# A three-part megakernel (attention, routed experts, Mamba): expert sums on GpSimd, one dt tile made in its own batch, two projections in halves

## The chip, the cores and the metric

The kernel runs on one core of a Trainium2 chip, in one launch. The metric is the time of one execution on the device in microseconds; the kernel before took 2910.95 us, the median of three runs (2910.9 to 2911.77).

## The reference, cut to what matters

All of it is float32. `x` has 16 batches of 512 tokens of width 256. The expert layer acts on the first 2048 tokens, that is on the first four batches.

```python
x = x + attention(layernorm(x))
x = x + experts(layernorm(x))     # first 2048 tokens, top 2 of 8, weighted sum of the two results
x = x + mamba(layernorm(x))       # all 16 batches
x = x + experts(layernorm(x))

def experts(x):                   # per token
    return sum(weight[k] * w2B[e_k].T @ w2A[e_k] @ gelu(w1B[e_k].T @ w1A[e_k] @ x) for k in range(2))

def mamba(x):                     # DI = 512 channels, N = 16 states, conv of 4 taps
    u, z = split(rmsnorm(x) @ in_proj)
    u = silu(causal_conv(u))
    dt_r, B, C = split(u @ x_proj)               # 64, 16, 16
    dt = softplus(dt_r @ dt_proj + bias)
    h[t] = exp(dt[t] * A) * h[t - 1] + dt[t] * B[t] * u[t]
    y = sum_n(h * C) + u * D
    return x + (y * silu(z)) @ out_proj
```

## The kernel before, in words

Four functions run one after another with a barrier between: `attention` (L55), `expert_ffn` (L436), `mamba` (L1018), `expert_ffn` again. The change lies in `mamba` alone. The first expert layer leaves its results as rows in DRAM; gathering a token's two rows, scaling them by its weights and adding them to `x` is done inside `mamba` by `fetch` and `add_experts`, two tiles of 128 tokens in each of the first eight batches (`XC` = 2, 16 tiles). `ORDER` puts the four batches that need them behind ten others.

**A batch is 32 units.** The 512 channels are four tiles `c` of 128 rows, and a tile's 16 states are eight pairs `n`; unit `i` = 8c + n. For each unit four engines work in turn on 128x1024 operands:
- ScalarE makes the decays exp(dt * A) (`decays`, L1549, two activations), two units ahead of the scan;
- the drive dt * B * u comes for even units from VectorE (`scale`, L1476: `ps_u` times `b_all`, into `ps_d[0]`), for odd units from TensorE (`drive`, L1808: `duT` against the diagonal matrices `bdiag`, into `ps_d[1]`);
- VectorE scans (L1488) into `state`, a ring of four;
- GpSimd multiplies by C (L1381, in place), and TensorE sums over the states by transposing into `ps_y` (`add_up`, L1821), two units later.

**Around the units** every engine's `emit(st)` loops over `i` and, at fixed numbers of `i`, does pieces of the neighbouring batches: `st.has(1)` is the batch ahead, `st.has(-1)` the one behind. TensorE's pieces are in the table `TURNS`, whose entries (kind, number, batch offset) run at the end of unit `i`: T transposes of the normalised input, U and Z the in-projection, V the convolution, X the x-projection, B the transposes of x-dbl, DT the dt-projection, DU transposes of dt * u, Y transposes of y, O the out-projection. All these results go to two PSUM banks in turn, `ps_f[0]` and `ps_f[1]`. `take` (L1710 on) makes a turn wait until the piece before it in the same bank has been read, by the table `OVER`:

```python
        OVER = {"T": (hT_ready, KT), "U": (up_ready, CT), "V": (u_ready, CT), "Z": (z_ready, CT),
                "X": (xd_ready, 1), "B": (bt_ready, 1), "DT": (dt_part, CT), "DU": (duT_ready, CT),
                "Y": (gated, CT), "O": (o_added, 2)}
```

**dt of a tile** passes through four engines: TensorE's DT, ScalarE's `softplus` (five activations and two table loads, L1561 to L1569), VectorE's `dt_relu` (L1443), GpSimd's `finish_dt` (L1352, L1355, L1360), which also makes `du` = dt * u. Then `du` is copied to `ps_u` by ScalarE (`put_du`, L1586), which `scale` of the tile's first unit waits for, and transposed by DU and copied to `duT` (`to_duT`, L1577), which the tile's first odd unit waits for. Softplus shares its buffers among tiles, so a tile's softplus waits for the finish of the one before. Tiles 0 and 1 are made in the batch ahead of their own, tiles 2 and 3 in their own.

**The residual.** The part of a batch's result that is not the mixer's (`x` plus its layernorm) is written by ScalarE into `xw` (L1681, at i = 25, two batches ahead), stored to `out`, loaded again one batch after its own units (L1270), and VectorE adds the two halves of O to it (L1506). `xw` is one buffer. The result is stored by SyncE (L1287), which counts `stored`, and ScalarE's next residual waits for it:

```python
                        if st.has(-1):
                            act.wait_ge(stored, 16 * (b - 2))
```

Other names: `gate` (L1460, L1464) adds u * D and multiplies by silu(z); `measure` (L1409) and `norm` (L1327 on) make the layernorm's numbers; `diagonal` makes one of the four parts of `bdiag`, two by GpSimd in the batch ahead (n = 1 and 3, L1369), two by ScalarE in its own (n = 5 and 7, L1596).

## Time and profile before

| | |
|---|---|
| median of three runs | 2910.95 us |
| profiled execution | 2913.27 us |
| span of its instructions | 2911.5 us |
| attention and first expert layer | to 798 us |
| units of the state-space stage (first to last scan) | 798.5 to 2640 us |
| last batch's rest and second expert layer | from 2640 us |
| TensorE busy (matmuls) | 2515.1 us, 86% of the span |
| VectorE busy | 2317.3 us, 80% |
| ScalarE busy | 1962.5 us, 67% |
| GpSimd busy | 1880.0 us, 65% |

How to read it: engines are PE (TensorE), DVE (VectorE), ACT (ScalarE), POOL (GpSimd) and SPq (SyncE's queue, which issues DMAs). L1488 is line 1488 of the kernel before. A timeline row gives the start from the span's first instruction, the time until the merged instructions end, how many they are (a float32 matmul counts twice), and in brackets how long the engine sat idle before them and what released it. Matmul durations are modelled with their tail, so consecutive rows overlap; the distance of two starts is the better measure. PEclk is the clock that TensorE was granted, 1.00 being 2.4 GHz and 0.50 being 1.2 GHz. A group's row gives busy time, the mean of one, and the idle time before.

### The profile page before, as it was taken

How to read it: one execution, taken by the hardware profiler on the slowest of the kernel's cores; microseconds unless marked ns; L12 is line 12 of the kernel's file. 1: busy time of each engine (PE TensorE's matmuls, PEld its weight loads, DVE VectorE, ACT ScalarE, POOL GpSimd, SP SyncE). 2: the span in 40 equal slices, each digit the busy share in tenths (PEclk: the TensorE clock that was granted, in tenths of full speed). 3: DMA queues.
4: the chain of work that ended last, by engine and by line, in shares of the span. 5: the costliest groups of instructions: out<-in, count | busy, mean ns of one | idle time of the engine just before them, and what ended most of it. 6: DMA issues, size and time to landing. Idle time of an engine off the chain costs nothing. (4 is left out here: it accounts for less than half of the span.)

```text
span 2911.5 us, 42446 instructions
## 1 busy us (share of the span) xinstructions
PE 2515.1 (86%) x15334; PEld 1943.2 (67%) x15334; DVE 2317.3 (80%) x2353; ACT 1962.5 (67%) x2845; POOL 1880.0 (65%) x1243
## 2 busy tenths in 40 slices
PE   5999998498698999999999999999999999974892
PEld 4878786365366767767777677777777777773561
DVE  6888784465189999999999999989988889894662
ACT  3655654154588788787787887877878878760451
POOL 1212121353279889888888888887888888883454
PEclk9999999699799999999999999999999999997996
DMA  1212110522313034033141330330312302304243
GB/s 50 66 43 65 43 58 29 125 76 64 99 61 124 27 106 128 9 127 103 30 131 27 106 124 9 109 109 10 117 38 80 117 9 102 103 1 113 74 103 105
DMA packets 144739, 219.74 MB, mean 75 GB/s; under 512 B 26980, under 2 KB 111844, under 8 KB 144548
## 3 DMA queue, kind: packets, MB, share of 16 engines
q1 hardware_dynamic: 137060, 196.78, 21.4%
q0 software_dynamic: 7488, 20.46, 2.7%
q8 instruction: 115, 1.88, 0.3%
q14 instruction: 76, 0.62, 0.1%
HBM read 174.69 MB, written 42.51 MB: 75 GB/s over the span
## 5 line engine op out<-in xcount | busy, mean ns | idle before, releaser
L1381 POOL TENSOR_TENSOR m_state<-m_state,m_c_all 128x1024 f32<-128x1024 f32 x512 | 1201.2, 2366 | 212.4 <-DVE m_state L1488 211.0
L1488 DVE TENSOR_TENSOR_SCAN m_state<-m_decay,m_ps_d 128x1024 f32<-128x1024 f32 x512 | 1150.9, 2273 | 76.6 <-PE m_ps_d L1808 55.9
L1549 ACT ACTIVATE m_decay<-m_dt,m_aneg 128x511 f32<-128x511 f32 x1024 | 659.2, 709 | 33.4 <-DVE m_state L1488 32.9
L1808 PEld LDWEIGHTS m_ps_d<-m_bdiag,m_duT 128*128 128x128 f32 x4096 | 512.0, 200 | 160.8 <-issue 92.4
L1808 PE MATMUL m_ps_d<-m_bdiag,m_duT 128*128 128x128 f32 x4096 | 530.5, 285 | 74.4 <-DVE m_state L1488 73.9
L1821 PE MATMUL m_ps_y<-m_ident,m_state 128*128 128x128 f32 x4096 | 525.3, 275 | 8.1 <-POOL m_state L1381 8.0
L1821 PEld LDWEIGHTS m_ps_y<-m_ident,m_state 128*128 128x128 f32 x4096 | 471.4, 143 | 82.2 <-issue 56.3
L1476 DVE TENSOR_TENSOR m_ps_d<-m_ps_u,m_b_all 128x1024 f32<-128x1024 f32 x256 | 315.4, 1232 | 35.2 <-ACT m_ps_u L1586 19.2
L1723 PE MATMUL m_ps_f<-m_hT,m_win 128*128 128x512 f32 x512 | 262.8, 640 | 47.2 <-DVE m_dt L1443 33.0
L1746 PE MATMUL m_ps_f<-m_up,m_tap 128*128 128x512 f32 x512 | 231.7, 596 | 0.0
L188 POOL TENSOR_TENSOR a_rstd<-a_var_eps,a_neg_half 128x4 f32<-128x4 f32 x16 | 16.2, 1010 | 297.5 <-DVE a_var_eps L277 297.5
L1723 PEld LDWEIGHTS m_ps_f<-m_hT,m_win 128*128 128x128 f32 x512 | 92.6, 201 | 130.3 <-issue 69.5
L900 ACT ACTIVATE f_hid<-f_ps_up 128x1024 f32<-128x1024 f32 x92 | 94.2, 1024 | 107.8 <-PE f_ps_up L968 107.8
L1746 PEld LDWEIGHTS m_ps_f<-m_up,m_tap 128*128 128x128 f32 x512 | 92.6, 190 | 97.8 <-issue 94.6
L1610 ACT ACTIVATE m_u<-m_ps_f,m_cb 128x512 f32<-128x512 f32 x64 | 44.0, 687 | 154.5 <-PE m_ps_f L1746 154.4
L194 POOL TENSOR_TENSOR a_trig_lo<-a_trig,a_trig_hi 128x2048 fp32r<-128x2048 f32 x16 | 73.7, 4608 | 96.5 <-ACT a_trig_hi L347 96.5
L424 PE MATMUL a_ps_o<-a_vals,a_probs 128*128 128x257 f32 x512 | 118.8, 385 | 16.3 <-DVE a_xout L290 14.5
L329 ACT ACTIVATE a_probs<-a_ps_s 128x512 f32<-128x512 f32 x64 | 38.3, 599 | 138.6 <-PE a_ps_s L401 138.5
L1352 POOL TENSOR_TENSOR m_sp_l<-m_sp_l,m_sp_a 128x512 f32<-128x512 f32 x64 | 81.6, 1275 | 72.6 <-ACT m_sp_a L1569 72.3
L1792 PE MATMUL m_ps_f<-m_wout,m_z 128*128 128x256 f32 x512 | 118.4, 385 | 2.5 <-DVE m_z L1464 1.7
L424 PEld LDWEIGHTS a_ps_o<-a_vals,a_probs 128*128 128x128 f32 x512 | 94.9, 190 | 37.4 <-DVE a_xout L290 19.7
L757 POOL TENSOR_TENSOR f_rstd<-f_var_eps,f_neg_half 128x2 f32<-128x2 f32 x46 | 33.2, 723 | 129.3 <-DVE f_var_eps L817 129.3
(203 smaller groups left out, 4367.5 us busy)
## 6 DMA issues: line engine op xcount, KB each, us to landing
m_c_all<-m_bc_rows SPq DMA_DIRECT2D x128, 512.0 KB, 7.4
m_b_all<-m_bc_rows SPq DMA_DIRECT2D x64, 512.0 KB, 8.0
out<-m_xw SPq DMA_DIRECT2D x32, 512.0 KB, 3.2
f_y_rows<-f_y_sb SPq DMA_DIRECT2D x46, 256.0 KB, 2.1
a_xin<-x SPq DMA_DIRECT2D x16, 512.0 KB, 4.6
a_xres<-x SPq DMA_DIRECT2D x16, 512.0 KB, 5.3
x<-a_xout SPq DMA_DIRECT2D x16, 512.0 KB, 3.3
m_xin<-x SPq DMA_DIRECT2D x16, 512.0 KB, 5.4
```

What stands on the lines that cost most here:

```text
L424: ins = nc.tensor.matmul(ps_o[r][:, 0:D + 1], probs[h][:, t, s * P:(s + 1) * P], vals[h][:, t, :], start=(t == 0), stop=(t == TT - 1))
L900: nc.scalar.activation(hid[q][:, :, :], ps_up[q][:, :, :], ACT.Gelu).then_inc(gelu_done, 1)
L1352: nc.gpsimd.tensor_tensor(sp_l[:, :], sp_l[:, :], sp_a[:, :], ALU.subtract).then_inc(sp_fix, 1)
L1381: nc.gpsimd.tensor_tensor(s, s, c_all[:, n, :, :], ALU.mult).then_inc(weighed, 1)
L1476: nc.vector.tensor_tensor(ps_d[0][:, :, :], ps_u[:, :].unsqueeze(1).to_broadcast([P, 2, S]), b_all[:, n // 2, :, :], ALU.mult).then_inc(sc ...
L1488: nc.vector.tensor_tensor_scan(state[:, r, :, :].rearrange("p n t -> p (n t)"), decay[:, r, :, :].rearrange("p n t -> p (n t)"), ps_d[i % ...
L1549: ins = nc.scalar.activation(decay[:, r, j, 1:S], dt_sb[:, c % DR, 1:S], ACT.Exp, scale=aneg[:, c, n:n + 1])
L1723: ins = nc.tensor.matmul(f[:, :], win[:, k, e * P:(e + 1) * P], hT[:, k, :], start=(k == 0), stop=(k == KT - 1))
L1746: ins = nc.tensor.matmul(f[:, :], tap[:, k, s, :], up[:, k % 2, s:s + S], start=(s == 0), stop=(s == K - 1))
L1792: ins = nc.tensor.matmul(f[:, v * D:(v + 1) * D], z_sb[h][:, c, t * P:(t + 1) * P], wout[:, c, :], start=(c == 0), stop=(c == CT - 1))
L1808: ins = nc.tensor.matmul(ps_d[1][:, j, t * P:(t + 1) * P], duT[:, c % DR, t, :], bdiag[:, n // 2, TT * j + t, :], start=True, stop=True)
L1821: ins = nc.tensor.matmul(ps_y[:, t, :], state[:, i % RING, j, t * P:(t + 1) * P], id_sb[:, :], start=(n == 0 and j == 0 and t == 0), stop= ...
```

## The change

1. `add_experts` moves from VectorE to GpSimd. On VectorE it was two fused multiply-adds per token tile (at i = 14 and 29); on GpSimd it is two multiplies by a column of weights and two adds (at i = 14 and 22). The gathers (`fetch`) move from i = 4 and 19 to 6 and 9.
2. dt of tile 1 is made at units 1 to 3 of its own batch instead of units 28 to 30 of the batch ahead: DT at 1, softplus at 1, `dt_relu` at 2, `finish_dt` at 3, DU at 5 (was 2), `put_du` at 6, `to_duT` at 7 (was 2).
3. O and X run in two halves in neighbouring units: O0 at 17 and 18 (was 17), X at 19 and 20 (was 19), O1 at 23 and 24 (was 23). VectorE's adds of O move from 18 and 24 to 19 and 25.
4. Around these: DT3, its softplus, `dt_relu` and `finish_dt` one unit later (15 to 18); Z0 and Z1 one unit later, and the silu of Z0 and Z1 from 25 to 27; gate 1 from 20 to 21; `measure` from 11 to 14, `norm` from 13 to 15; part 5 of `bdiag` by GpSimd at unit 0 instead of ScalarE, part 7 at 4 instead of 3. With 30 turns as before, the banks are dealt out anew by the order of the table.

```diff
@@ TURNS
         0: [("T", 0, 1), ("T", 1, 1)],
-        2: [("DU", 1, 0), ("U", 0, 1)],
+        1: [("DT", 1, 0)],
+        2: [("U", 0, 1)],
         3: [("Y", 3, -1), ("U", 1, 1)],
-        5: [("V", 0, 1)],
+        5: [("DU", 1, 0), ("V", 0, 1)],
...
-        15: [("DT", 3, 0)],
+        16: [("DT", 3, 0)],
         17: [("O", 0, -1)],
+        18: [("O", 0, -1)],
         19: [("X", 0, 1)],
-        20: [("Y", 1, 0), ("DU", 3, 0)],
+        20: [("X", 0, 1), ("Y", 1, 0), ("DU", 3, 0)],
         21: [("B", 0, 1)],
         22: [("DT", 0, 1)],
         23: [("O", 1, -1)],
-        24: [("Z", 0, 1)],
-        25: [("Z", 1, 1)],
-        26: [("DU", 0, 1)],
+        24: [("O", 1, -1)],
+        25: [("Z", 0, 1)],
+        26: [("Z", 1, 1), ("DU", 0, 1)],
         27: [("Y", 2, 0)],
-        28: [("DT", 1, 1)],
@@ gpsimd
+            def add_experts(t):
+
+                r = t % (2 * XC)
+                pool.wait_ge(ex_loaded[t // XC % 2], 16 * XC * (t // XC // 2 + 1))
+                if t == 0:
+                    pool.wait_ge(ex_weights, 16)
+                pool.wait_ge(ex_got[t % XC], 16 * TOPK * (t // XC + 1))
+                for k in range(TOPK):
+                    y = ex_y[t % XC][k]
+                    nc.gpsimd.tensor_scalar(y[:, :], y[:, :], tok_w[:, t, k:k + 1], None,
+                                            ALU.mult).then_inc(ex_weighed, 1)
+                pool.wait_ge(ex_weighed, 3 * t + 2)
+                nc.gpsimd.tensor_tensor(ex_x[:, r, :], ex_y[t % XC][0][:, :], ex_x[:, r, :],
+                                        ALU.add).then_inc(ex_weighed, 1)
+                pool.wait_ge(ex_weighed, 3 * t + 3)
+                nc.gpsimd.tensor_tensor(ex_x[:, r, :], ex_y[t % XC][1][:, :], ex_x[:, r, :],
+                                        ALU.add).then_inc(ex_added, 1)
...
-                    if i in (10, 17) and st.has(0):
+                    if i == 0 and st.has(0):
+                        diagonal(st, 0, 5)
+                    if i in (3, 10, 18) and st.has(0):
                         finish_dt(st, 0, i // 8 + 1)
-                    if i in (24, 30) and st.has(1):
-                        finish_dt(st, 1, (24, 30).index(i))
+                    if i == 24 and st.has(1):
+                        finish_dt(st, 1, 0)
...
-                    if i == 13 and st.has(2):
+                    if i == 15 and st.has(2):
                         norm(st)
-                    if i in (4, 19) and st.has(0) and st.item(0) < NTK // XC:
-                        fetch(XC * st.item(0) + (4, 19).index(i))
+                    if i in (6, 9) and st.has(0) and st.item(0) < NTK // XC:
+                        fetch(XC * st.item(0) + (6, 9).index(i))
+                    if i in (14, 22) and st.has(0) and st.item(0) < NTK // XC:
+                        add_experts(XC * st.item(0) + (14, 22).index(i))
@@ vector
-            def add_experts(t):
...
-                nc.vector.scalar_tensor_tensor(out=ex_x[:, r, :], in0=ex_y[t % XC][0][:, :], scalar=tok_w[:, t, 0:1],
-                                               in1=ex_x[:, r, :], op0=ALU.mult, op1=ALU.add).then_inc(ex_weighed, 1)
-                dve.wait_ge(ex_weighed, t + 1)
-                nc.vector.scalar_tensor_tensor(out=ex_x[:, r, :], in0=ex_y[t % XC][1][:, :], scalar=tok_w[:, t, 1:2],
-                                               in1=ex_x[:, r, :], op0=ALU.mult, op1=ALU.add).then_inc(ex_added, 1)
...
-                    if i in (18, 24) and st.has(-1):
-                        b, v = st.item(-1), (i - 18) // 6
+                    if i in (19, 25) and st.has(-1):
+                        b, v = st.item(-1), (i - 19) // 6
...
-                    if i in (12, 20, 28) and st.has(0):
+                    if i in (12, 21, 28) and st.has(0):
                         gate(st, 0, (i - 12) // 8)
-                    if i == 11 and st.has(2) and st.has(1):
+                    if i == 14 and st.has(2) and st.has(1):
...
@@ scalar
-                    if i in (9, 16) and st.has(0):
+                    if i in (1, 9, 17) and st.has(0):
                         softplus(st, 0, i // 8 + 1)
...
-                    if i in (25, 30) and st.has(1):
-                        silu(st, z_sb, "Z", z_full, z_ready, (0, 1) if i == 25 else (2, 3))
-                    if i in (2, 12, 21) and st.has(0):
-                        to_duT(st, 0, 1 + (2, 12, 21).index(i))
+                    if i in (27, 30) and st.has(1):
+                        silu(st, z_sb, "Z", z_full, z_ready, (0, 1) if i == 27 else (2, 3))
+                    if i in (7, 12, 21) and st.has(0):
+                        to_duT(st, 0, 1 + (7, 12, 21).index(i))
...
-                    if i in (23, 29) and st.has(1):
-                        softplus(st, 1, (23, 29).index(i))
+                    if i == 23 and st.has(1):
+                        softplus(st, 1, 0)
@@ tensor, turn: X (O alike, with one 128-token column half a part)
+                parts = HALVES[kind, k, o]
+                part, last = parts.index(i), i == parts[-1]
...
-                    f = take(st, kind, k)
-                    if not st.has(0):
-                        pe.wait_ge(v_loaded, 16 * 2)
-                    pe.wait_ge(u_ready, CT * (b + 1))
-                    for c in range(CT):
+                    f = f_bank(kind, k)
+                    if part == 0:
+                        take(st, kind, k)
+                        if not st.has(0):
+                            pe.wait_ge(v_loaded, 16 * 2)
+                        pe.wait_ge(u_ready, CT * (b + 1))
+                    for c in range(2 * part, 2 * part + 2):
                         ins = nc.tensor.matmul(f[0:RX, :], wx[:, c, :], u_sb[h][:, c, :],
-                                               start=(c == 0), stop=(c == CT - 1))
-                    ins.then_inc(x_full, 1)
+                                               start=(c == 0), stop=(c == CT - 1), skip_group_check=True)
+                    if last:
+                        ins.then_inc(x_full, 1)
```

What this does to the order on three places follows, of a batch in the middle of the stage.

ScalarE at the end of a batch (units 24 to 28), before: m_z is the silu of Z, m_xw the residual, m_duT the copy of the transposed du.

```order
L1549 ACTIVATE m_decay<-m_dt,m_aneg 128x511 x4
L1610 ACT_TABLE_LOAD
L1610 ACTIVATE m_z<-m_ps_f 128x512 x2
L1612 ACT_TABLE_LOAD
L1681 ACTIVATE m_xw<-m_xin,m_res_shift,m_res_scale 128x256 x4
L1549 ACTIVATE m_decay<-m_dt,m_aneg 128x511 x4
L1577 ACTIVATE m_duT<-m_ps_f 128x512
L1549 ACTIVATE m_decay<-m_dt,m_aneg 128x511 x2
L1686 ACTIVATE m_xin<-m_xin,m_h_shift,m_h_scale 128x256 x4
```

The same place after the change:

```order
L1558 ACTIVATE m_decay<-m_dt,m_aneg 128x511 x4
L1690 ACTIVATE m_xw<-m_xin,m_res_shift,m_res_scale 128x256 x4
L1558 ACTIVATE m_decay<-m_dt,m_aneg 128x511 x4
L1619 ACT_TABLE_LOAD
L1619 ACTIVATE m_z<-m_ps_f 128x512 x2
L1621 ACT_TABLE_LOAD
L1558 ACTIVATE m_decay<-m_dt,m_aneg 128x511 x2
L1586 ACTIVATE m_duT<-m_ps_f 128x512
L1695 ACTIVATE m_xin<-m_xin,m_h_shift,m_h_scale 128x256 x4
```

The silu of Z0 and Z1 stood ahead of the residual and now stands behind it and four more decays.

ScalarE at the head of a batch (units 31 to 3), before: m_hT is the copy of the T transposes, m_up that of U, m_bdiag part 5 of the diagonal.

```order
L1549 ACTIVATE m_decay<-m_dt,m_aneg 128x511 x4
L1626 ACTIVATE m_hT<-m_ps_f,m_nw 128x512 x2
L1596 ACTIVATE m_bdiag<-m_ident,m_bt 128x128 x8
L1549 ACTIVATE m_decay<-m_dt,m_aneg 128x511 x4
L1637 ACTIVATE m_up<-m_ps_f 128x512
L1577 ACTIVATE m_duT<-m_ps_f 128x512
L1549 ACTIVATE m_decay<-m_dt,m_aneg 128x511 x2
L1637 ACTIVATE m_up<-m_ps_f 128x512
```

The same place after:

```order
L1558 ACTIVATE m_decay<-m_dt,m_aneg 128x511 x4
L1635 ACTIVATE m_hT<-m_ps_f,m_nw 128x512 x2
L1558 ACTIVATE m_decay<-m_dt,m_aneg 128x511 x2
L1570 ACTIVATE m_sp_a<-m_ps_f 128x512
L1572 ACTIVATE m_sp_e<-m_sp_a 128x512
L1574 ACTIVATE m_sp_a<-m_sp_e 128x512
L1576 ACT_TABLE_LOAD
L1576 ACTIVATE m_sp_l<-m_sp_a 128x512
L1577 ACT_TABLE_LOAD
L1578 ACTIVATE m_sp_a<-m_sp_a 128x512
L1558 ACTIVATE m_decay<-m_dt,m_aneg 128x511 x2
L1646 ACTIVATE m_up<-m_ps_f 128x512
```

Softplus of tile 1 (m_sp_a to m_sp_a) now stands between the copy of T and the copy of U0; part 5 of the diagonal and the copy of the transposed du are gone from here.

TensorE in the middle of a batch (units 15 to 20), before: the pieces with m_wdt, m_wout and m_wx are DT3, O0 and X, m_ps_d is a drive, m_ps_y a sum (x16 is two units' sums).

```order
L1770 MATMUL m_ps_f<-m_xd,m_wdt 128x512
L1808 MATMUL m_ps_d<-m_bdiag,m_duT 128x128 x8
L1821 MATMUL m_ps_y<-m_ident,m_state 128x128 x16
L1792 MATMUL m_ps_f<-m_wout,m_z 128x256 x8
L1808 MATMUL m_ps_d<-m_bdiag,m_duT 128x128 x8
L1821 MATMUL m_ps_y<-m_ident,m_state 128x128 x16
L1755 MATMUL m_ps_f<-m_u,m_wx 96x512 x4
L1808 MATMUL m_ps_d<-m_bdiag,m_duT 128x128 x8
L1821 MATMUL m_ps_y<-m_ident,m_state 128x128 x8
L1783 MATMUL m_ps_f<-m_ident,m_y 128x128 x4
```

The same place after:

```order
L1824 MATMUL m_ps_d<-m_bdiag,m_duT 128x128 x8
L1837 MATMUL m_ps_y<-m_ident,m_state 128x128 x8
L1784 MATMUL m_ps_f<-m_xd,m_wdt 128x512
L1837 MATMUL m_ps_y<-m_ident,m_state 128x128 x8
L1807 MATMUL m_ps_f<-m_wout,m_z 128x256 x4
L1824 MATMUL m_ps_d<-m_bdiag,m_duT 128x128 x8
L1837 MATMUL m_ps_y<-m_ident,m_state 128x128 x8
L1807 MATMUL m_ps_f<-m_wout,m_z 128x256 x4
L1837 MATMUL m_ps_y<-m_ident,m_state 128x128 x8
L1768 MATMUL m_ps_f<-m_u,m_wx 96x512 x2
L1824 MATMUL m_ps_d<-m_bdiag,m_duT 128x128 x8
L1837 MATMUL m_ps_y<-m_ident,m_state 128x128 x8
```

DT3 came before the drive of unit 17 and now comes after it and a sum; between two sums there is now at most half of O0 or X.

## Rows read from the trace of the kernel before

**Rows 1.** Windows, two stretches; columns: stretch, us, busy per engine, PEclk, DMA share, GB/s

```profile
800.00:1728.00 928.00, 852.50 (x5268) 656.22 (x5269) 854.81 (x619) 757.58 (x1185) 807.12 (x486) 0.98 0.26 84
...
1960.20:1963.00 2.80, 2.71 (x13) 2.74 (x14) 2.70 (x2) 2.77 (x5) 2.80 (x3) 0.53 0.98 350
```

**Rows 2.** Timeline, VectorE, stage start and batch 9: start us, us, work, [idle before <-releaser]

```profile
797.21 1.23 DVE L1476 TENSOR_TENSOR m_ps_d<-m_ps_u,m_b_all 128x1024 f32<-128x1024 f32 x1 [4.34 <-ACT m_ps_u L1586]
...
1841.08 4.46 DVE L1488 TENSOR_TENSOR_SCAN m_state<-m_decay,m_ps_d 128x1024 f32<-128x1024 f32 x2
...
1873.97 2.29 DVE L1488 TENSOR_TENSOR_SCAN m_state<-m_decay,m_ps_d 128x1024 f32<-128x1024 f32 x1 [1.24 <-PE m_ps_d L1808]
...
1903.49 2.29 DVE L1488 TENSOR_TENSOR_SCAN m_state<-m_decay,m_ps_d 128x1024 f32<-128x1024 f32 x1 [2.10 <-PE m_ps_d L1808]
...
1911.42 4.46 DVE L1488 TENSOR_TENSOR_SCAN m_state<-m_decay,m_ps_d 128x1024 f32<-128x1024 f32 x2 [0.42 <-ACT m_decay L1549]
...
1918.69 0.76 DVE L1460 SCALAR_TENSOR_TENSOR m_ps_f<-m_u,m_dsk,m_ps_f 128x512 f32<-128x512 f32 x1 [1.54 <-PE m_ps_f L1783]
...
1925.99 4.46 DVE L1488 TENSOR_TENSOR_SCAN m_state<-m_decay,m_ps_d 128x1024 f32<-128x1024 f32 x2
...
1932.29 0.69 DVE L1506 TENSOR_TENSOR m_xw<-m_xw,m_ps_f 128x512 f32<-128x512 f32 x1 [0.56 <-PE m_ps_f L1792]
...
1956.72 1.23 DVE L1476 TENSOR_TENSOR m_ps_d<-m_ps_u,m_b_all 128x1024 f32<-128x1024 f32 x1 [2.41 <-ACT m_ps_u L1586]
1957.87 4.46 DVE L1488 TENSOR_TENSOR_SCAN m_state<-m_decay,m_ps_d 128x1024 f32<-128x1024 f32 x2
```

**Rows 3.** Timeline, TensorE, batch 9

```profile
1843.50 3.04 PE L1808 MATMUL m_ps_d<-m_bdiag,m_duT 128*128 128x128 f32 x16 [3.06 <-DVE m_state L1488]
...
1856.28 1.88 PE L1723 MATMUL m_ps_f<-m_hT,m_win 128*128 128x512 f32 x4
...
1936.39 1.04 PE L1821 MATMUL m_ps_y<-m_ident,m_state 128*128 128x128 f32 x8
1937.26 1.88 PE L1723 MATMUL m_ps_f<-m_hT,m_win 128*128 128x512 f32 x4
1938.98 1.95 PE L1808 MATMUL m_ps_d<-m_bdiag,m_duT 128*128 128x128 f32 x16
```

**Rows 4.** Timeline, ScalarE, batch 9

```profile
1848.52 1.26 ACT L1626 ACTIVATE m_hT<-m_ps_f,m_nw 128x512 f32<-128x512 f32 x2 [1.09 <-PE m_ps_f L1740]
...
1875.65 0.60 ACT L1561 ACTIVATE m_sp_a<-m_ps_f 128x512 f32<-128x512 f32 x1 [0.18 <-PE m_ps_f L1770]
...
1877.59 1.28 ACT L1567 ACT_TABLE_LOAD   x1
1878.88 0.63 ACT L1567 ACTIVATE m_sp_l<-m_sp_a 128x512 f32<-128x512 f32 x1
...
1881.36 0.58 ACT L1637 ACTIVATE m_up<-m_ps_f 128x512 f32<-128x512 f32 x1
...
1901.91 2.56 ACT L1549 ACTIVATE m_decay<-m_dt,m_aneg 128x511 f32<-128x511 f32 x4
...
1941.09 2.08 ACT L1681 ACTIVATE m_xw<-m_xin,m_res_shift,m_res_scale 128x256 f32<-128x256 f32 x4
```

**Rows 5.** Timeline, SyncE's queue, batch 9

```profile
1933.00 0.39 SPq L1287 DMA_DIRECT2D out<-m_xw  x1
```

**Rows 6.** DMA issues by line: xcount, KB each, median us to landing

```profile
out<-m_xw SPq DMA_DIRECT2D x32, 512.0 KB, 3.2
```

**Rows 7.** GpSimd's groups: busy us, mean ns | idle before

```profile
L1352 POOL TENSOR_TENSOR m_sp_l<-m_sp_l,m_sp_a 128x512 f32<-128x512 f32 x64 | 81.6, 1275 | 72.6 <-ACT m_sp_a L1569 72.3
...
L1318 POOL DMA_INDIRECT m_ex_y<-f_y_rows,m_places x32 | 31.4, 983 | 7.3 <-issue 6.3
...
L763 POOL COPY f_s_1a<-f_w_1a 128x256 f32 x46 | 18.5, 402 | 0.6 <-issue 0.2
```

**Rows 8.** One line, L1433: ns min/median/max, first and last start us

```profile
L1433 DVE SCALAR_TENSOR_TENSOR m_ex_x<-m_ex_y,m_tok_w,m_ex_x x16: 485/1472/2470, 853.6 to 1719.9; 128x256 f32<-128x256 f32 x16
```

50 lines of the change are left out of this document (23 added, 27 removed).

## The prediction

> **What bounds the kernel now.** I read the windows first, then the timelines of VectorE, TensorE and ScalarE through one batch, then GpSimd's groups. The long stretch is the state-space stage: 928 us for its first eight batches [rows 1], 116.0 us each. VectorE is busy in 854.81 of these, TensorE in 852.50, GpSimd in 807.12. No engine is full; each batch loses 9 us of VectorE's time in waits at fixed places. Batch 9 has no expert adds and still takes 116.8: from the second scan of the pair at 1841.08, that is 1843.27, to 1957.87 + 2.19 = 1960.06 [rows 2]. So time taken off VectorE alone is worth nothing here; waits fill the hole. What counts is the chain through the named waits.
>
> In batch 9 I cut at scans 9, 17 and 23 [rows 2]: 30.7 us to scan 9 (ended by a wait of 1.24 for TensorE's drive matmuls), 29.5 us to scan 17 (a wait of 2.10 for the same), 22.5 us to scan 23 (0.42 for a decay, 1.54 for the Y transposes), 34.1 us to the next batch (2.41 for the copy into ps_u; I take 33.3 as the average, since the mean batch is 0.8 shorter than batch 9). Pieces of TensorE work are told by the distance of their starts: 0.87 a sum into ps_y, 1.72 a pair of 512-wide matmuls; a drive lasts 1.95, of which I count 1.8, and four transposes half a sum [rows 3]. The working below gives the new length of each stretch.
>
> **Head of the batch, scan 0 to 9: 30.7 becomes 33.8.** The dt of tile 1 moves here: a 0.86 us matmul (half of a pair), ScalarE's softplus, 0.6 us on VectorE, 3.9 us on GpSimd (three rows of 1.27 with their gaps). The softplus costs ScalarE 5.7 us, from 1875.65 to 1881.36, with two table loads of 1.28 in it [rows 4]. It now stands ahead of the copy of U0 into up, and U1's matmul waits for that copy. Chain from the boundary: T transposes done at 4.5 (before it was 5.2 [rows 4]; the low clock after the idle 3.06 us [rows 3] goes, since TensorE now arrives at the boundary without idling), hT 1.0, decays 1.25, softplus 5.7, decays 1.25, copy 0.55: U1 can start at 14.3. It started at 1856.28, 13.0 after the boundary [rows 3], and from there to scan 9 went 17.7 us, all TensorE work, to which tile 1's du transposes (moved from unit 2 to 5) add 0.44. That gives 32.5. TensorE stands idle 2.4 us before U1. After the idle 3.06 us at the boundary the granted clock was 0.53 for the next 2.8 us [rows 1], the 1.2 GHz level, and the 1.7 us of work there took twice as long; I charge 1.3, three chances in four of 1.7. That GpSimd takes over one part of bdiag delays nothing: it waits for scans at this place, and ScalarE sheds the part after the copy's critical hT, where it is covered by the softplus.
>
> The Trainium skill ("ScalarE: Activation LUTs", what ACT_TABLE_LOAD costs) gives about 2.66 us for each switch, load and drain together; the rows show 1.28 and the next activation 0.01 later. By the page each of fifteen softplus would hold the copy 2.8 us longer and the whole would come to some 2947 us; the rows decide.
>
> **Scan 9 to 17: 29.5 becomes 29.1 without experts, 30.3 with.** DT3's 0.86 us leaves the path before drive 17, and the wait there was 2.10. But ScalarE is right behind: the decays of unit 17, behind V3's silu and its table load, begin at 1901.91 and end at 1903.2, 0.3 ahead of the scan [rows 2, 4]. So DT3's move gives 0.3 to 0.4, not 0.9. In batches 0 to 7 the second gather (two issues of 0.98 with gaps, 2.3 us [rows 7]) now stands before finish_dt of tile 2, whose du the transposes wait for: 1.2 later, net +0.8. VectorE's measure moves behind scale 16, which has room.
>
> **Scan 17 to 23: 22.5 becomes 20.1.** The gate moves from 20 to 21, behind Y1, and softplus 3 behind two more decays: the waits of 1.54 and 0.42 go, and with halves of 1.7 us no drive is held by a block of 3.4. VectorE's own work is all that is left. The Y1, DU3 and B transposes still wait only for what is done.
>
> **Scan 23 to the boundary: 33.3 becomes 32.7.** Here two savings meet a new wait. Saved: softplus 1 before the copy into ps_u (the 2.41), dt_relu 0.7, and with experts the late add. New: ScalarE writes the next residual into xw only once the store of xw has landed. Before, VectorE's second output add ended at 1932.97, the store was issued at 1933.00 [rows 5] and takes 3.2 us [rows 6], and ScalarE came at 1941.09 [rows 4], after Z's silu. Now the add comes one unit later, and silu two units later, behind the residual. Counted from scan 23: VectorE runs scans 23 to 25 (2.2 each), a scale (1.2), dt_relu, y_read and the add (0.6 each to the next start), ending at 9.8 with the gaps; the store lands at 13.1. ScalarE is there at 9.0 and stands 4 us. Then residual 2.1, four decays 2.5, table 1.3, silu 0.65: Z0 at 19.6. TensorE has its Z1 at 14.7 and next the du transposes, whose PSUM bank Z0's silu must free: 5 us idle, and the clock falls (+1.7). Y2 is done at 23.1, the gate at 24.5, drive 29 at 24.9; two scans, a scale and scan 31 end at 32.7. Without this wait the stretch would be 28. It holds in batches 1 to 13; batch 0 has no store, 14 no residual, and they get 5.1 and 3.5.
>
> **Expert adds.** VectorE loses 32 instructions. The second of each pair, L1433, takes 0.49 at least and 2.47 at most, 1.47 in the median [rows 8]; the first of a pair I put at 0.49. That is 3.9 us a batch, all of it inside the stretches above. GpSimd gets four instructions a token tile. Its 128x512 tensor_tensor takes 1.27, so 0.64 for 128x256; its 128x256 copy takes 0.40 [rows 7]. No row has the scalar multiply. Its ends are 0.40, the copy, and 1.27, two inputs at twice the size; I take 0.5, since one input and a column of scalars are nearest to the copy: 2.5 us a tile, 5 a batch. GpSimd goes from 101 to about 108 of 116 us, its part of bdiag with it, and at DU3 I find it 3 us ahead of TensorE. The Trainium skill ("GPSIMD Engine Reference", Engine selection) puts elementwise work on VectorE, GpSimd being about twice as slow with two inputs; by that alone the move would cost 8 x (5 - 3.9) = 9 us.
>
> **The sum**, against the profiled execution of 2913.3 us (span 2911.5), which is 2.3 above the median of the runs:
> - start of the stage: the copy into ps_u comes without softplus 1 before it; VectorE waited 4.34 for it [rows 2]: -3.9 (ends 0 and -4.3, the load of b following close);
> - head, batches 1 to 14: 14 x 3.1 = +43; batch 0 +1, batch 15 +0.6;
> - scans 9 to 17: 8 x 0.8 - 7 x 0.4 = +3.6;
> - scans 17 to 23: 15 x -2.3 = -34;
> - tail: 13 x -0.7 = -9; batches 0 and 14 -5.1 - 3.5 = -8.6.
>
> Together -7.3: 2906.0 us by the profiled run, 2903.7 by the median. Chains of this kind gain some hundredths at each hand-over that I left out, so I say 2905.5, all but no change. About 0.2%, 5.8 us, is what can be told from none.
>
> **Rivals.**
> 1. The clock stays up before U1: 14 x 1.3 less, and some of the tail's fall overlaps with idle time, 10 us: about 2877. For it: TensorE idles only 2.4 us where the rows show the low clock after 3.06. Chance 0.22.
> 2. Slower: the head binds harder. Z3 now ends at the boundary itself, its silu and table load delay the decays of units 1 and 2, and these the hT copies; U1 is another 1.2 us late in 14 batches, +17: 2923. It decides as soon as those decays end more than 4.5 us after the boundary, where I have them at 4.4. Against it: batches 8 to 13 have slack in GpSimd. Chance 0.26.
> 3. The store is no wait, because ScalarE arrives late anyway: 13 x 4.6 off, 2845. The order speaks against it. Chance 0.05.
> 4. GpSimd becomes the bound in the eight expert batches (a multiply of 1.27 us each: 32 x 0.8 = 26, half of it hidden): +13, 2919. This is also where the skill's rule on elementwise work would lead. Chance 0.07.
>
> The forecast itself has 0.40, with a range of its own from 2892 to 2918. The range of 2876 to 2932 takes in rivals 1, 2 and 4. Faster by over 0.2%: rivals 1 and 3 and under half of the forecast's case, 0.45; within 0.2%: 0.27; slower: 0.28.
>
> **What would show it.** Right: a VectorE wait of about 3 us before the gate of unit 28 for the Y transposes, TensorE idle 5 us before L1790 behind Z's silu, ScalarE idle 4 us before the residual; TensorE idle 2 to 3 us before the second U matmul with the clock low behind it; no wait before the gate of unit 21. Wrong: a batch under 112 or over 118 us; no idle time before the residual; GpSimd releasing TensorE's sums in batches 0 to 7.

## The result and the profile after

| | before | after |
|---|---|---|
| median of the runs, us | 2910.93 (2905.88 to 2911.77, 4 runs) | 2922.72 (2921.17 to 2926.16, 4 runs) |
| profiled execution, span, us | 2911.5 | 2920.3 |
| mean granted clock of TensorE | 0.947 | 0.943 |

The ratio is 1.0045, with a 95% interval of 1.0033 to 1.0057: 0.45% slower. The forecast was 2905.5, a little faster; the time lies inside the range of 2876 to 2932, on the other side of no change. The page of after gives, for the engines and for the lines that the prediction spoke of (columns as on the page: busy, mean ns, idle time before and who ended it):

```profile
PE 2508.0 (86%) x15334; PEld 1948.9 (67%) x15334; DVE 2286.7 (78%) x2321; ACT 1918.6 (66%) x2717; POOL 1956.6 (67%) x1323
...
L1499 DVE TENSOR_TENSOR_SCAN m_state<-m_decay,m_ps_d 128x1024 f32<-128x1024 f32 x512 | 1153.4, 2274 | 130.5 <-ACT m_decay L1558 69.2
...
L1732 PE MATMUL m_ps_f<-m_hT,m_win 128*128 128x512 f32 x512 | 262.6, 639 | 45.8 <-ACT m_up L1646 34.2
...
L1790 PE MATMUL m_ps_f<-m_ident,m_du 128*128 128x128 f32 x256 | 47.7, 317 | 108.6 <-ACT m_z L1619 62.1
...
out<-m_xw SPq DMA_DIRECT2D x32, 512.0 KB, 2.9
```

TensorE waits 62.1 us in all for Z's silu before the du transposes, and 34.2 us for the copy into `up` before the second U matmul: two waits that the prediction named.

**Batch 9, cut as in [rows 2].** VectorE's timeline of after (start us, us, work, idle before and its releaser). Scan 0 is the second of the first row's pair:

```profile
1854.73 4.46 DVE L1499 TENSOR_TENSOR_SCAN m_state<-m_decay,m_ps_d 128x1024 f32<-128x1024 f32 x2
...
1890.99 2.29 DVE L1499 TENSOR_TENSOR_SCAN m_state<-m_decay,m_ps_d 128x1024 f32<-128x1024 f32 x1 [1.23 <-PE m_ps_d L1824]
...
1920.14 2.29 DVE L1499 TENSOR_TENSOR_SCAN m_state<-m_decay,m_ps_d 128x1024 f32<-128x1024 f32 x1 [1.41 <-ACT m_decay L1558]
...
1935.56 0.75 DVE L1471 SCALAR_TENSOR_TENSOR m_ps_f<-m_u,m_dsk,m_ps_f 128x512 f32<-128x512 f32 x1
...
1940.48 4.45 DVE L1499 TENSOR_TENSOR_SCAN m_state<-m_decay,m_ps_d 128x1024 f32<-128x1024 f32 x2
...
1963.37 0.76 DVE L1471 SCALAR_TENSOR_TENSOR m_ps_f<-m_u,m_dsk,m_ps_f 128x512 f32<-128x512 f32 x1 [3.07 <-PE m_ps_f L1797]
...
1971.13 4.46 DVE L1499 TENSOR_TENSOR_SCAN m_state<-m_decay,m_ps_d 128x1024 f32<-128x1024 f32 x2
```

Scan 0 at 1854.73 + 2.19 = 1856.92, scan 9 at 1890.99 (34.1 us), scan 17 at 1920.14 (29.1), scan 23 at 1940.48 (20.3), next scan 0 at 1973.32 (32.8). The forecast was 33.8, 29.1, 20.1, 32.7. The gate of unit 21 (1935.56) has no wait any more where [rows 2] had 1.54, and the gate of unit 28 waits 3.07 for the Y transposes.

**Batch 5, with experts**, in four engines' timelines. First TensorE: before U1, before tile 2's du transposes, and before the next batch's first du transposes.

```profile
1395.87 2.71 PE L1732 MATMUL m_ps_f<-m_hT,m_win 128*128 128x512 f32 x4 [2.29 <-ACT m_up L1646]
...
1429.32 0.63 PE L1790 MATMUL m_ps_f<-m_ident,m_du 128*128 128x128 f32 x4 [2.92 <-POOL m_du L1380]
...
1486.48 1.11 PE L1790 MATMUL m_ps_f<-m_ident,m_du 128*128 128x128 f32 x4 [4.74 <-ACT m_z L1619]
```

In batch 9, which has no gather, the middle one of these waits is 1.5 us shorter:

```profile
1903.05 0.63 PE L1790 MATMUL m_ps_f<-m_ident,m_du 128*128 128x128 f32 x4 [1.41 <-POOL m_du L1380]
```

ScalarE in batch 5, at the residual and Z's silu behind it:

```profile
1479.99 2.08 ACT L1690 ACTIVATE m_xw<-m_xin,m_res_shift,m_res_scale 128x256 f32<-128x256 f32 x4 [4.23 <-issue]
1481.97 2.54 ACT L1558 ACTIVATE m_decay<-m_dt,m_aneg 128x511 f32<-128x511 f32 x4
1484.53 1.28 ACT L1619 ACT_TABLE_LOAD   x1
1485.83 1.08 ACT L1619 ACTIVATE m_z<-m_ps_f 128x512 f32<-128x512 f32 x2
```

SyncE's queue, the store that it waits for:

```profile
1476.99 0.39 SPq L1289 DMA_DIRECT2D out<-m_xw  x1
```

1476.99 plus 2.9, the median to landing, is 1479.9, and the residual starts at 1479.99. GpSimd, at the second tile's expert adds and the work queued behind them:

```profile
1468.72 1.84 POOL L1333 TENSOR_SCALAR m_ex_y<-m_ex_y,m_tok_w 128x256 f32<-128x256 f32 x2
1470.64 0.72 POOL L1336 TENSOR_TENSOR m_ex_x<-m_ex_y,m_ex_x 128x256 f32<-128x256 f32 x1
1471.44 0.73 POOL L1339 TENSOR_TENSOR m_ex_x<-m_ex_y,m_ex_x 128x256 f32<-128x256 f32 x1
1472.13 4.69 POOL L1401 TENSOR_TENSOR m_state<-m_state,m_c_all 128x1024 f32<-128x1024 f32 x2
1476.77 1.27 POOL L1372 TENSOR_TENSOR m_sp_l<-m_sp_l,m_sp_a 128x512 f32<-128x512 f32 x1
```

The multiply takes 0.92 us each, 1.84 a tile, where the prediction took 0.5. No row has an idle time before it: GpSimd works without a pause from 1434.2 to 1493.7. The windows of the two batches (batch 5, batch 9; columns: stretch, length, busy time of TensorE, its weight loads, VectorE, ScalarE and GpSimd, granted clock, DMA) show the difference:

```profile
1381.70:1501.10 119.40, 108.66 (x670) 85.61 (x669) 103.76 (x75) 91.84 (x141) 109.22 (x70) 0.96 0.26 79
1856.80:1973.20 116.40, 107.26 (x670) 84.06 (x669) 103.81 (x75) 91.88 (x141) 98.88 (x58) 0.97 0.23 74
```

VectorE and ScalarE do the same work in both. GpSimd has 10.3 us more in the expert batch, and that batch is 3.0 us longer than batch 9: 1.5 in scans 9 to 17 (30.66 against 29.15) and 1.6 from scan 23 on (34.41 against 32.85). Before, batches 2 to 7, with experts, took 116.1 us and batches 8 to 13, without, 116.0.

**Where the 8.8 us of span came from**, by the sum's own terms (start times of all 512 scans, profiled executions). The stretch from scan 23 to the next batch's first scan is called the tail from here on.

| term | forecast | measured |
|---|---|---|
| start of the stage | -3.9 | -4.7 |
| head, scan 0 to 9 | +44.6 | +41.9 |
| scan 9 to 17 | +3.6 | +9.7 |
| scan 17 to 23 | -34 | -30.8 |
| scan 23 to the boundary | -17.6 | -4.4 |
| after the last scan | 0 | -2.9 |
| sum | -7.3 | +8.8 |

### The profile page after: what moved, and what is told of

Same layout as the page of the kernel before. It is cut to its first block and busy times, and to the rows that moved or that the text cites. A ratio compares the mean times of both kernels' runs of the same rounds, so it can differ in the third digit from the quotient of the medians.

```text
span 2920.3 us, 42368 instructions
## 1 busy us (share of the span) xinstructions
PE 2508.0 (86%) x15334; PEld 1948.9 (67%) x15334; DVE 2286.7 (78%) x2321; ACT 1918.6 (66%) x2717; POOL 1956.6 (67%) x1323
## 5 line engine op out<-in xcount | busy, mean ns | idle before, releaser
L1837 PE MATMUL m_ps_y<-m_ident,m_state 128*128 128x128 f32 x4096 | 533.5, 277 | 11.3 <-POOL m_state L1401 10.4
L1824 PE MATMUL m_ps_d<-m_bdiag,m_duT 128*128 128x128 f32 x4096 | 521.3, 282 | 16.6 <-DVE m_state L1499 16.5
L1732 PE MATMUL m_ps_f<-m_hT,m_win 128*128 128x512 f32 x512 | 262.6, 639 | 45.8 <-ACT m_up L1646 34.2
L1790 PE MATMUL m_ps_f<-m_ident,m_du 128*128 128x128 f32 x256 | 47.7, 317 | 108.6 <-ACT m_z L1619 62.1
L1807 PE MATMUL m_ps_f<-m_wout,m_z 128*128 128x256 f32 x512 | 122.9, 384 | 2.5 <-DVE m_z L1475 1.7
L757 POOL TENSOR_TENSOR f_rstd<-f_var_eps,f_neg_half 128x2 f32<-128x2 f32 x46 | 33.4, 725 | 128.0 <-DVE f_var_eps L817 128.0
```

The source lines that it names most:

```text
L1732: ins = nc.tensor.matmul(f[:, :], win[:, k, e * P:(e + 1) * P], hT[:, k, :], start=(k == 0), stop=(k == KT - 1))
L1807: ins = nc.tensor.matmul(f[:, part * D:(part + 1) * D], z_sb[h][:, c, t * P:(t + 1) * P], wout[:, c, :], start=(c == 0), stop=(c == CT - 1))
L1824: ins = nc.tensor.matmul(ps_d[1][:, j, t * P:(t + 1) * P], duT[:, c % DR, t, :], bdiag[:, n // 2, TT * j + t, :], start=True, stop=True)
L1837: ins = nc.tensor.matmul(ps_y[:, t, :], state[:, i % RING, j, t * P:(t + 1) * P], id_sb[:, :], start=(n == 0 and j == 0 and t == 0), stop= ...
```

## The experiments

Fourteen kernels were run beside the kernel before and the change. A ratio is always to the kernel before, run at the same time, with its 95% interval. The table has the mean length of each stretch in their profiled executions, first over batches 2 to 7 (with experts), then over 8 to 13 (without); the short names are explained below.

| kernel | 0-9 | 9-17 | 17-23 | tail | batch | 0-9 | 9-17 | 17-23 | tail | batch |
|---|---|---|---|---|---|---|---|---|---|---|
| before | 30.6 | 29.5 | 22.4 | 33.6 | 116.1 | 30.7 | 29.5 | 22.4 | 33.4 | 116.0 |
| after | 33.5 | 30.7 | 20.3 | 34.2 | 118.6 | 33.8 | 29.0 | 20.3 | 33.0 | 116.2 |
| silu first | 32.7 | 31.7 | 20.3 | 32.0 | 116.7 | 33.6 | 29.0 | 20.3 | 31.8 | 114.8 |
| dt 1 ahead | 30.4 | 32.3 | 20.3 | 36.4 | 119.5 | 30.6 | 29.0 | 20.3 | 36.1 | 116.0 |
| adds on VectorE | 33.8 | 31.5 | 23.1 | 33.5 | 121.8 | 33.7 | 29.1 | 20.3 | 32.9 | 116.1 |
| both | 31.3 | 31.5 | 20.3 | 34.6 | 117.7 | 31.1 | 29.0 | 20.3 | 34.4 | 114.9 |
| store behind | 33.7 | 31.8 | 20.3 | 30.5 | 116.3 | 33.5 | 29.0 | 20.3 | 28.7 | 111.5 |
| gather later | 34.1 | 29.1 | 21.7 | 34.6 | 119.4 | 33.8 | 29.0 | 20.3 | 32.9 | 116.1 |
| copy first | 35.8 | 32.3 | 20.3 | 34.5 | 122.9 | 34.4 | 29.0 | 20.3 | 32.6 | 116.3 |
| part 1 alone | 30.6 | 32.5 | 23.8 | 32.6 | 119.5 | 30.8 | 29.5 | 22.5 | 33.3 | 116.0 |
| no multiply | 34.0 | 32.0 | 20.3 | 33.2 | 119.5 | 33.5 | 29.0 | 20.3 | 33.0 | 115.9 |
| adds in the head | 35.6 | 28.7 | 20.3 | 29.6 | 114.2 | 33.0 | 29.1 | 20.3 | 28.7 | 111.1 |
| the same, dt 1 ahead | 33.6 | 28.7 | 20.3 | 35.3 | 117.9 | 31.1 | 29.1 | 20.3 | 34.4 | 114.9 |
| part 3 alone | 30.4 | 29.3 | 20.3 | 37.6 | 117.7 | 30.5 | 29.3 | 20.3 | 36.1 | 116.3 |
| later, no multiply | 33.8 | 29.1 | 20.3 | 32.9 | 116.1 | 33.8 | 29.0 | 20.3 | 32.9 | 116.1 |
| adds apart | 33.9 | 28.7 | 20.3 | 29.6 | 112.5 | 33.1 | 29.1 | 20.3 | 28.7 | 111.1 |

### Silu first: the wait for the store taken off TensorE's path

```diff
-                    if i in (27, 30) and st.has(1):
+                    if i in (26, 30) and st.has(1):      # Z's silu
-                    if i == 25 and st.has(2):
+                    if i == 27 and st.has(2):            # the residual
```

> The change, but ScalarE takes Z's first silu at unit 26, ahead of the residual, which goes to unit 27. Theory (the residual waits for the store, and Z's silu behind it holds TensorE): no idle time of TensorE over 1 us before L1790 in units 25 to 29, stretch from scan 23 to the boundary 28.5 to 30 us in place of 32.9 (34.4 with experts); 13 batches, so 45 to 60 us off, 2865 to 2878. Rival (the 4.7 us are hidden behind VectorE or GpSimd anyway): less than 15 us off, over 2907.

Measured: 2913.05 us, ratio to before 0.9999 [0.9989, 1.0009]. TensorE's wait is gone and so is VectorE's at the gate of unit 28, but the tail is 31.8 and not 29. The time is in the rival's range (over 2907), but not for the rival's reason: the wait was not hidden, another took its place. VectorE's timeline (batch 5) has a new wait, and SyncE's queue shows why:

```profile
1503.91 1.23 DVE L1487 TENSOR_TENSOR m_ps_d<-m_ps_u,m_b_all 128x1024 f32<-128x1024 f32 x1 [3.51 <-DMA m_b_all<-m_bc_rows]
```

```profile
1495.59 0.38 SPq L1293 DMA_DIRECT2D out<-m_xw  x1
1496.09 0.43 SPq L1242 DMA_DIRECT2D m_c_all<-m_bc_rows  x1
1496.57 0.95 SPq L1247 DMA_DIRECT2D m_b_all<-m_bc_rows  x1
```

SyncE waits for the residual before it issues the residual's store, and the next batch's loads of B and C stand behind that store in its queue. The residual now ends at 1495.6, so the first load of B is issued at 1496.57 and the next batch's first `scale` waits for it. The forecast forgot the queue behind the moved step.

### Store behind: that queue put right

```diff
-                if st.has(2):                                   # ahead of the loads of B and C
-                    b = st.item(2)
-                    sp.wait_ge(res_made, b + 1)
-                    sp.dma_start(rows(out, b), xw[:, :, :]).then_inc(res_stored, 16)
...
                         if n % 2 == 0:
                             b_pair(n // 2)
+                if st.has(2):                                   # the same four lines, behind them
...
```

> The kernel with Z's silu ahead of the residual, and in SP's queue the residual's store moved behind the next batch's loads of B and C. Theory (there the first scale of a batch waited 3.6 us for the load into b_all, which stood in SP's queue behind the late residual's store): no DMA wait before the last scale of a batch, tail 28 to 29.5 in place of 31.7; about 2870 to 2885. Rival (the loads are late for another reason, the C rows' store or the queue's own time): tail stays over 31, total over 2905.

Measured: 2881.25 us, 0.9890 [0.9874, 0.9907], inside the theory's range. The tail is 28.7 us in batches 8 to 13, the wait for `b_all` is gone, and what is left is short: VectorE's timeline in batch 9 has

```profile
1950.33 1.23 DVE L1487 TENSOR_TENSOR m_ps_d<-m_ps_u,m_b_all 128x1024 f32<-128x1024 f32 x1 [0.59 <-ACT m_ps_u L1595]
```

So the prediction's "without this wait the stretch would be 28" holds to 0.7 us, but only with the second wait behind it removed as well. The expert batches gained much less (116.3 against 111.5).

### Is it GpSimd's queue? Gather later, no multiply, and both

The expert batches differ from the others by the gather's issues, the adds and their transfers. The first run only moves the second gather:

```diff
-                    if i in (6, 9) and st.has(0) and st.item(0) < NTK // XC:
-                        fetch(XC * st.item(0) + (6, 9).index(i))
+                    if i in (6, 11) and st.has(0) and st.item(0) < NTK // XC:
+                        fetch(XC * st.item(0) + (6, 11).index(i))
```

> The change, but the second gather is issued at GpSimd's unit 11, behind finish_dt of tile 2, not at 9 ahead of it. Theory (the gather's two issues ahead of finish_dt hold du and its transposes): scan 9 to 17 of batches 2 to 7 from 30.66 to 29.1 us, 10 to 13 us off in all, 2908 to 2913. Rival (the expert adds or a shared port lengthen that stretch): it stays over 30.4, total over 2918.

Measured: 2928.82 us, 1.0058 [1.0041, 1.0075]. Scans 9 to 17 fell to 29.1 as expected, so the 1.6 us there are the gather's. But scans 17 to 23 rose by 1.4, heads and tails by 0.6 and 0.4, and the total was over the theory's range. GpSimd is now late a few units on: in each of batches 1 to 7 TensorE waits 1.2 us for it before a sum that it did not wait for in the change. TensorE's timeline of this kernel in batch 5:

```profile
1458.85 1.09 PE L1837 MATMUL m_ps_y<-m_ident,m_state 128*128 128x128 f32 x8 [1.18 <-POOL m_state L1401]
```

The second run leaves the multiplies out of `add_experts`, so the expert rows are added without their weights:

```diff
-                for k in range(TOPK):
-                    y = ex_y[t % XC][k]
-                    nc.gpsimd.tensor_scalar(y[:, :], y[:, :], tok_w[:, t, k:k + 1], None,
-                                            ALU.mult).then_inc(ex_weighed, 1)
```

> The change without the two multiplies by the routing weight (the expert rows are added unweighted), so GpSimd has 3.7 us less a batch in batches 0 to 7 and nothing else moves. Theory (in expert batches GpSimd runs without a pause from unit 12 to 28, and its finish_dt of the next tile 0 and its last weightings come 4.5 us later than in batch 9): tail of batches 3 to 7 from 34.4 to 32.9 to 33.6 us, total 8 to 14 us off, 2909 to 2915. Rival (the longer expert batches are due to the gather and to the low clock alone): under 4 us off, over 2918.

Measured: 2925.44 us, 1.0049 [1.0032, 1.0066]. The tail of batches 3 to 5 fell from 34.4 to 32.85, as the theory wanted (batch 2 had 32.9 in both; batch 6 rose to 35.1), and the total didn't fall: scans 9 to 17 went from 30.7 to 32.3 in batches 2 to 6, a place that the edit doesn't touch. TensorE's timeline of this kernel, batch 5, at tile 2's du transposes:

```profile
1432.62 0.63 PE L1785 MATMUL m_ps_f<-m_ident,m_du 128*128 128x128 f32 x4 [2.91 <-POOL m_du L1375]
1433.08 3.50 PE L1819 MATMUL m_ps_d<-m_bdiag,m_duT 128*128 128x128 f32 x16
```

and windows of 2 us from that point, of this kernel,

```profile
1433.10:1435.10 2.00, 2.00 (x13) 2.00 (x12) 0.28 (x1) 1.82 (x4) 2.00 (x2) 0.53 0.00 0
1435.10:1437.10 2.00, 2.00 (x13) 2.00 (x13) 0.43 (x1) 1.98 (x4) 2.00 (x1) 0.62 0.00 0
```

and of after:

```profile
1429.70:1431.70 2.00, 2.00 (x21) 2.00 (x20) 0.37 (x1) 1.72 (x3) 2.00 (x2) 1.00 0.03 8
1431.70:1433.70 2.00, 2.00 (x18) 1.81 (x17) 1.87 (x1) 1.98 (x5) 2.00 (x1) 1.00 0.00 0
```

The idle time is the same, 2.91 and 2.92 us. In one kernel the granted clock behind it is 0.53 to 0.62, the 1.2 GHz level, and the drive takes 3.50 us; in the other it stays at 1.00, 2.4 GHz, and the drive takes 1.95. That is the 1.6 us. So this run took one load away and met the low clock at another place. The third takes both away (the two edits above together):

> The change with the second gather at GpSimd's unit 11 and without the two multiplies by the routing weight (rows are added unweighted). Theory (the whole extra of an expert batch is GpSimd's queue: the gather ahead of finish_dt makes TensorE idle 2.9 us, at times with the clock low behind, and the adds make GpSimd late for the tail; each run that took one away got the other): batches 1 to 7 of 116.2 to 117.2 us, like 9 to 13, total 2896 to 2906. Rival (the adds and the transfers cost something of their own): batches 2 to 7 over 118, total over 2912.

Measured: 2902.25 us, 0.9972 [0.9962, 0.9983]. Batches 2 to 7 and 8 to 13 are now alike, 116.1 us each, stretch by stretch. The windows of batches 3 and 9:

```profile
1140.90:1257.30 116.40, 107.35 (x671) 84.15 (x670) 103.93 (x75) 92.00 (x141) 105.58 (x66) 0.97 0.26 83
1837.50:1953.60 116.10, 107.05 (x671) 83.98 (x670) 103.82 (x75) 91.89 (x141) 98.89 (x58) 0.97 0.23 74
```

GpSimd still has 6.7 us more in batch 3, the gathers, adds and transfers all remain, and the batch is no longer. The rival, a cost of the gathers, the adds and the transfers themselves, falls; the theory holds, and in this arrangement 105.6 us of GpSimd's work a batch fit where 109.2 don't. The run takes out more than the forecast had wrong (the whole multiply, 0.92 us, where it had counted 0.5), so it does not show what multiplies of 0.5 us would have given.

### The three parts, each alone or undone

**Adds on VectorE.** The change with `add_experts` of the kernel before called on VectorE at i = 14 and 22 (gathers at 6 and 9):

```diff
-                    if i in (14, 22) and ...:            # in GpSimd's emit
-                        add_experts(...)
+                    if i in (14, 22) and ...:            # in VectorE's emit
+                        add_experts(...)
```

> The change, but the expert adds are on VectorE again, at the same units 14 and 22. Theory (the adds on GpSimd cost nothing of their own, the expert batches are longer for the low clock behind the 4.7 us idle): stretch 17 to 23 longer by 1 to 2 us, scan 9 to 17 shorter by up to 1, tail of batches 3 to 7 stays over 34; total within 6 us of the change. Rival (GpSimd is the bound in expert batches: 6.8 us more of it a batch): batches 3 to 7 fall from 119.4 to 116.5 to 117.5, total 16 to 24 us off, about 2900.

Measured: 2940.70 us, 1.0093 [1.0076, 1.0110], 18 us over the change: theory and rival both missed. Scans 17 to 23, where VectorE's own work is all that is left, grew by 2.8 us a batch, and GpSimd's relief gave nothing back in scans 9 to 17, where it is the gather that counts. At these units it is right to have the adds off VectorE. The Trainium skill ("GPSIMD Engine Reference", Engine selection) prefers VectorE for them; this run speaks against it at these units. At others it is different: the fastest run below has the adds on VectorE, where it waits anyway.

**Part 1 alone**, in the kernel before (adds on GpSimd at 14 and 22, gathers at 6 and 9):

```diff
-                    if i in (4, 19) and ...:             # fetch
+                    if i in (6, 9) and ...:
...
+                    if i in (14, 22) and ...:            # add_experts, from VectorE's (14, 29)
```

> The kernel before with one part of the change alone: expert adds on GpSimd at units 14 and 22 and both gathers at 6 and 9. Theory A (GpSimd's adds are hidden, the gather costs 1.1 to 1.6 us in scans 9 to 17, the late add on VectorE at 29 gives back 0.6): 2912 to 2920. Theory B (the mirror of the run with the adds back on VectorE, which was 18 us slower): 2890 to 2898. Theory C (GpSimd's 6.8 us a batch bind): over 2925.

Measured: 2936.32 us, 1.0085 [1.0068, 1.0102], as theory C had it: 25 us over before, by scans 9 to 17 (+3.0 a batch in 2 to 7) and 17 to 23 (+1.4). TensorE's timeline in batch 5 shows the same wait of 2.9 us, and the drive behind it takes 3.14 us, not 1.95:

```profile
1441.06 1.09 PE L1781 MATMUL m_ps_f<-m_ident,m_du 128*128 128x128 f32 x4 [2.93 <-POOL m_du L1378]
1441.94 3.14 PE L1813 MATMUL m_ps_d<-m_bdiag,m_duT 128*128 128x128 f32 x16
```

**Part 3 alone**: the halves, with the steps that follow them (output adds at 19 and 25, gate at 21, Z's turns at 25 and 26, its silu at 27, DT3 at 16 and softplus 3 at 17), and the part of `bdiag` on GpSimd; adds and dt 1 as before.

```diff
         17: [("O", 0, -1)],
+        18: [("O", 0, -1)],
         19: [("X", 0, 1)],
-        20: [("Y", 1, 0), ("DU", 3, 0)],
+        20: [("X", 0, 1), ("Y", 1, 0), ("DU", 3, 0)],
```

> The kernel before with the third part alone: O and X in halves, with the output adds, the second gate, Z's turns and silu and the softplus of tile 3 where the change has them; the expert adds on VectorE at 14 and 29 and the dt of tile 1 in the batch ahead, as before. Theory: scans 17 to 23 20.3 us in place of 22.3, paid back by the tail, where the residual waits for the store (36 us in place of 33.3): 2915 to 2930. Rival (the tail's wait needs the dt of tile 1 or the experts' move): tail at or under 33.5, total 2880 to 2890.

Measured: 2917.82 us, 1.0023 [1.0013, 1.0033]. Scans 17 to 23 gain 2.1 us a batch and the tail loses 2.8 in batches 8 to 13 and 4.0 in batches 2 to 7, as the theory had it. The wait for the store comes with this part: in batch 9 ScalarE stands 3.92 us before the residual, and TensorE is idle 4.74 us before the du transposes, for Z's silu, here too.

**Dt 1 ahead**: the change without part 2, that is `("DT", 1, 1)` at unit 28 and its softplus, dt and finish at 29 and 30 again.

```diff
-        1: [("DT", 1, 0)],
...
+        28: [("DT", 1, 1)],
...
-                    if i in (1, 9, 17) and st.has(0):
+                    if i in (9, 17) and st.has(0):       # softplus; and (23, 29) for the batch ahead
```

> The change, but the dt of tile 1 is made in the batch ahead as in the kernel before (units 28 to 30). Theory (softplus 1 ahead of the copy of U0 costs the head 3.3 us a batch): scan 0 to 9 back to 30.5 to 30.9 us in place of 34.0; the tail gets softplus 1 back ahead of the copy into ps_u and grows by 2 to 4 us, so all but cancels: 2905 to 2925. Rival (the head is longer for the later du transposes or for GpSimd's part of bdiag, not for the softplus): head stays over 33, total over 2950.

Measured: 2938.50 us, 1.0086 [1.0069, 1.0103]. In batches 8 to 13 the head gives back 3.2 us and the tail takes 3.1: a zero sum, as expected. In the expert batches scans 9 to 17 took 32.3 and the tail 36.4, and the whole was 16 us slower than the change, outside the theory's range. Of the 16 us, 6.9 stand before the first scan (800.8 against 793.9 us), where softplus 1 stands ahead of the copy into `ps_u` again. Scans 9 to 17 are the low clock again: the drive behind TensorE's 2.9 us of idle time takes 3.3 to 3.6 us in all eight expert batches, in the change 3.1 to 3.4 in batches 0 and 1 and 1.95 in the others.

**Copy first**: the softplus of tile 1 moved behind the copy of U0, to take the prediction's 3.1 us off the head.

```diff
-                    if i in (1, 9, 17) and st.has(0):
+                    if i in (9, 17) and st.has(0):
                         softplus(st, 0, i // 8 + 1)
...
+                    if i == 2 and st.has(0):             # behind the copy into up
+                        softplus(st, 0, 1)
```

> The change, but ScalarE makes the softplus of tile 1 behind the copy of U0 into up (unit 2) and VectorE its dt at unit 3. Theory (the copy behind the softplus holds U1 and with it the head): TensorE's idle time of 2.3 us before U1 and the low clock behind it go, U1 starts 4 to 5 us sooner, scan 0 to 9 falls from 34.0 to 31 to 32.5; 14 batches, 2880 to 2900. Rival (the head is bound by tile 1's own chain, softplus, dt, du, copy into ps_u, which now starts later): head 34 to 36, total 2920 to 2950.

Measured: 2952.41 us, 1.0136 [1.0119, 1.0153]. The rival was right, with a total 2 us above its range: VectorE's timeline of batch 9 shows tile 1's own chain as the next bound, a `scale` waiting for the copy into `ps_u` and the scan behind it for the drive.

```profile
1915.33 1.23 DVE L1487 TENSOR_TENSOR m_ps_d<-m_ps_u,m_b_all 128x1024 f32<-128x1024 f32 x1 [2.51 <-ACT m_ps_u L1595]
1917.32 4.46 DVE L1499 TENSOR_TENSOR_SCAN m_state<-m_decay,m_ps_d 128x1024 f32<-128x1024 f32 x2 [0.76 <-PE m_ps_d L1826]
```

### Towards a version that beats both

**Both**: silu first and dt 1 ahead, the store where it was.

```diff
+        28: [("DT", 1, 1)],                              # and its softplus, dt and finish at 29, 30
...
+                    if i in (26, 30) and st.has(1):      # Z's silu
+                    if i == 27 and st.has(2):            # the residual
```

> Both: Z's first silu ahead of the residual, and the dt of tile 1 in the batch ahead. Theory: head 30.5 to 30.9, tail 30 to 32.5, so batches of 109.5 to 113 us and 2825 to 2865 in all, below the kernel before. Rival (with the dt's softplus back, the tail is what it was before, 33.3, since ScalarE's own work bounds it): 2880 to 2890, the kernel before less its gain in scans 17 to 23.

Measured: 2916.86 us, 1.0020 [1.0010, 1.0030]; head 31.1, tail 34.4 without experts. Neither range held it: in batches 8 to 13 the dt's place made no difference yet (114.9 against 114.8 of silu first).

**Adds in the head**: silu first, store behind, the adds on VectorE at units 5 and 8, the gathers on GpSimd one batch ahead at 11 and 19.

```diff
-                    if i in (6, 9) and st.has(0) and st.item(0) < NTK // XC:
-                        fetch(XC * st.item(0) + (6, 9).index(i))
+                    if i in (11, 19) and st.has(1) and st.item(1) < NTK // XC:
+                        fetch(XC * st.item(1) + (11, 19).index(i))
...
+                    if i in (5, 8) and st.has(0) and st.item(0) < NTK // XC:     # VectorE
+                        add_experts(XC * st.item(0) + (5, 8).index(i))
```

> Z's silu ahead of the residual, the residual's store behind the loads, and the expert adds on VectorE at units 5 and 8, where it waits for the drives, with the gathers issued one batch ahead at GpSimd's units 11 and 19. Theory (adds hide in VectorE's waits of the head, GpSimd is unloaded): expert batches within 1.5 us of the others, 110.5 to 113 us each; 2840 to 2860. Rival (the adds lengthen the head by their own 2 us, or the gather's issues cost as much in their new place): 2865 to 2885, no gain over the run with the store behind the loads.

Measured: 2862.64 us, 0.9830 [0.9814, 0.9847]. GpSimd's load is out of the way (28.7 in scans 9 to 17), but the heads with adds are 2.6 us longer than those without (35.6 against 33.0). With **dt 1 ahead** of its batch on top of this (the same edit as above),

> As the run with the adds in the head, but the dt of tile 1 made in the batch ahead as in the kernel before. Theory (moving it into the batch itself costs the head 1.5 to 3.3 us and gives the tail 2.4 back, so it is nearly neutral once the store is out of the way): head 30.4 to 31, tail 30.5 to 32.5, total within 10 us of that run, 2845 to 2865. Rival (softplus 1 is what fills ScalarE before the boundary): tail over 33.5, 2880 or more.

it took 2913.61 us, 1.0010 [1.0000, 1.0020]: the rival was right, the head gains 2 us and the tail loses 5.7. VectorE's timeline at the end of batch 9 shows ScalarE's softplus ahead of the boundary:

```profile
1965.21 0.69 DVE L1447 SCALAR_TENSOR_TENSOR m_dt<-m_ps_f,m_sp_e 128x512 f32<-128x512 f32 x1 [1.25 <-ACT m_sp_e L1567]
1970.25 1.23 DVE L1480 TENSOR_TENSOR m_ps_d<-m_ps_u,m_b_all 128x1024 f32<-128x1024 f32 x1 [4.34 <-ACT m_ps_u L1590]
```

So, without experts, part 2 is worth 3.8 us a batch (114.9 against 111.1) once neither Z's silu nor the loads of B and C wait for the residual and its store, and nothing in the change as it was made (116.0 against 116.2). In the change's expert batches it was worth 0.8 us (119.5 against 118.6).

**Adds apart**: the four adds one by one.

```diff
-                    if i in (5, 8) and st.has(0) and st.item(0) < NTK // XC:
-                        add_experts(XC * st.item(0) + (5, 8).index(i))
+                    if i in (3, 4, 6, 8) and st.has(0) and st.item(0) < NTK // XC:
+                        add_expert(XC * st.item(0) + i // 5, i in (4, 8))
```

> As the run with the adds in the head, but the four adds one by one behind scans 3, 4, 6 and 8. Theory (each falls into a wait of VectorE for a decay or a drive): expert batches 112 to 114 us in place of 114.4, total 2845 to 2860. Rival (the adds' own 1.1 and 1.5 us come on top wherever they stand): 2858 to 2867.

Measured: 2848.48 us, 0.9788 [0.9772, 0.9804], 62 us under before and 74 under the change. The adds are mostly hidden in VectorE's waits: the windows of batches 5 and 9 have 107.76 and 103.45 us of VectorE's work, 4.3 more with the adds, and are 112.7 and 110.3 us long. In the mean the expert batches are 1.4 us longer than the others.

## Why the prediction missed

**What was right.** The places of the waits that it named and all four stretches without experts: 33.8, 29.0, 20.3 and 33.0 us against 33.8, 29.1, 20.1 and 32.7. TensorE idles 2.29 us before U1 and mostly finds the low clock behind: from the start of U1 to the end of the drive after it, 5.3 to 5.5 us pass in ten of batches 1 to 14 and 3.8 in the other four. ScalarE stands 3.9 to 4.2 us before the residual (4 foretold), TensorE 4.74 before the du transposes (5 foretold), VectorE 3.1 to 3.3 before the gate of unit 28 (3). Batches 8 to 13 came to 116.2 where the terms gave 115.7.

Rival 1, the clock staying up before U1, happened in these four only, behind the same 2.3 us of idle time: batches 1, 2, 3 and 12, with heads of 32.9, 32.4, 32.4 and 32.7 us against 34.0 in the ten. Rival 2 had the sign, not the cause: the head was not longer than forecast. Rival 3 didn't come: the store is a wait. Of the signs of being wrong one came clearly, a batch over 118 us (batch 1 and batches 4 to 7, 118.7 to 119.5); GpSimd released TensorE's sums after more than a few tenths of waiting in batch 0 alone (three waits, 6.0 us).

**The step that failed** is the costing of the expert adds: "GpSimd goes from 101 to about 108 of 116 us ... and at DU3 I find it 3 us ahead of TensorE". Two sizes in it were wrong, and one conclusion: that this load would be hidden. Its total was nearly right (109.2 us measured in batch 5) and so was the check at DU3, where TensorE has no wait for GpSimd; the cost came elsewhere.
1. The multiply was taken at 0.5 us and takes 0.92 in all 32, so GpSimd gets 3.4 us a tile instead of 2.5. Between ends of 0.40 and 1.27 the middle, 0.84, would have been nearer.
2. The second gather ahead of `finish_dt` was put at 1.2 us (30.3 with experts against 29.1 without). It cost 1.6 in batches 2 to 7 and 3.2 in batches 0 and 1, in scans 9 to 17: 5.9 us of the miss over eight batches. The second 1.6 is the low clock: the drive behind the wait takes 3.1 and 3.4 us there and 1.95 in the others.
3. The engine was checked at DU3 and not behind the second adds, at unit 22. In batch 5 the finish of the next batch's tile 0 starts at 1476.77, 95.0 us after the batch's first scan, in batch 9 it starts 90.5 after. The tail of expert batches came to 34.2 and not 32.7. Directly it costs 0.3 us, by which the output add, the store and the residual come later. The rest is TensorE's clock behind its idle 4.74 us: windows of 2 us from 1485.7 on have 0.51, 0.50, 0.50 and 0.79 granted, in batch 9 from 1958.9 on 0.82, 0.50, 0.83 and 1.00, and from the start of the du transposes to the end of the drive behind them 6.7 us pass against 5.4. In batches 0 to 7 the tail explains 10.3 us of the miss, 1.9 of them in batch 0, whose tail was forecast 5.1 us shorter than before and came out 3.2 shorter.

How much of this is GpSimd's doing stays open. Batches 2 and 3 of the same execution have the same idle time at the same place, 19.8 us after scan 23 (19.4 in batch 9), and the drive behind it takes 1.95 us in one and 3.16 in the other; the tails are 32.9 and 34.4. TensorE's timeline:

```profile
1131.37 1.12 PE L1790 MATMUL m_ps_f<-m_ident,m_du 128*128 128x128 f32 x4 [4.74 <-ACT m_z L1619]
...
1134.51 1.95 PE L1824 MATMUL m_ps_d<-m_bdiag,m_duT 128*128 128x128 f32 x16
...
1247.62 1.12 PE L1790 MATMUL m_ps_f<-m_ident,m_du 128*128 128x128 f32 x4 [4.74 <-ACT m_z L1619]
...
1251.09 3.16 PE L1824 MATMUL m_ps_d<-m_bdiag,m_duT 128*128 128x128 f32 x16
```

So the 0.3 us are GpSimd's. The 1.3 us of clock in batches 3 to 7 went away in the runs without the multiplies (but for batch 6 of the first and batch 5 of the second), and why the clock stays low longer in one batch than in another is not shown.

The gather and the tail are together 16 us, which is the miss, 8.8 against -7.3 of span. The other differences (3.2 us less gained in scans 17 to 23, 2.7 less lost in the head, 2.9 gained after the last scan and 0.8 at the start, 2.9 more in the tails of batches 8 to 14) cancel to under a microsecond, which is luck. The run with both loads taken off GpSimd shows the sum of the two: expert batches as long as the others, and 2902.25 us, 20 under the change. That this is 3 us from the forecast is in part luck too, since it leaves the multiplies out altogether. Rival 4, with 0.07, was nearest to what came: GpSimd too late in the expert batches, 2919. It asked for a multiply of 1.27, half of it hidden, and 0.92 was enough. It should have had more weight, since the sum looked at an engine with 108 of 116 us of work in one place only.

The 3.9 us a batch that VectorE loses were taken to lie "inside the stretches", which was loose: where the change has made VectorE the bound, in scans 17 to 23, they cost their full 2.8 us a batch.

## What to carry to other kernels

When a step is put on an engine with little slack, follow that engine's queue through the whole period and compare each hand-over behind the step with one period that lacks it, not only the next one. A step that waits for a transfer should stand behind everything that doesn't need it, on its engine and in the queue that issues the transfer: here moving the residual behind Z's silu gained 10 us, and its store behind the loads another 32. A part that looks neutral can be worth much once another is gone: in batches without experts dt 1 in its own batch gained nothing while another wait covered it, and 3.8 us afterwards.

## What was not expected of the hardware

- GpSimd's multiply of 128x256 by a column of scalars takes 0.92 us, more than its two-input add of the same size, 0.72. The Trainium skill ("GPSIMD Engine Reference", Engine selection) says that operations with one input run at about line rate there and those with two at half; the rows show the reverse order.
- The same idle time of TensorE, 2.9 us, was followed by the 1.2 GHz level in one kernel and by 2.4 GHz in another, and the stretch behind was 1.6 us longer or not: scans 9 to 17 of batches with that wait took 30.7 or 32.3. The 2.3 us before U1 did the same within one execution of the change: the granted clock behind them falls to 0.50 in batch 5 and stays at 1.00 in batch 2, with heads of 34.0 and 32.4. An edit elsewhere shifts which it is, so a stretch is judged better over several batches than by one. The Trainium skill ("TensorE: Matmul & The Clock Gate", Part 1) says that the number of slow matmuls differs between runs of one kernel; here it also differs between batches of one run. By its advice not to fit to that number it would be left out; in the heads alone it was worth some 16 us, ten batches of 34.0 against 32.4.
- VectorE's scaled add of 128x256 took 0.46 to 2.47 us with the same shapes [rows 8]. In the trace of before the second add of a pair takes 0.485 us in the eight places where GpSimd works on 128x4 operands beside it, and 2.46 to 2.47 in the eight where GpSimd's multiply of 128x1024 runs for 2.2 us of it. So the place of such an add decides its price.
